# Neighbourhood attention and a mixture of experts: keys and queries copied from their staging tiles straight into the matmul operands, with six key slots

## What is computed

```python
# block 1: 7x7 neighbourhood attention, 12 heads of 32, 16 register tokens
qkv = _gn(x) @ qkv_w.T + qkv_b                  # group norm, 32 groups
reg_kv = registers @ qkv_w[384:].T + qkv_b[384:]
scores = q . concat(k, reg_k) / sqrt(32)        # masked: 7x7 window + 16 registers
x = x + softmax(scores) @ concat(v, reg_v) @ out_w.T + out_b
# block 2: mixture of 4 experts, top 2, hidden width 96
combine = top-2 weights of softmax(xn @ router_w.T + router_b), renormalised
h = gelu(xn @ fc1_w.T + fc1_b)                  # exact gelu, xn = _gn(x)
x = x + (h * combine) @ fc2_w + combine @ fc2_b
```

## Time and profile before

| what | us |
|---|---|
| three runs of the kernel | 646.35, 649.06, 655.0 (median 649.06) |
| span of the profiled execution (first to last instruction) | 648.7 |
| PE busy in it | 570.3 (88%) |
| DVE busy | 447.4 (69%) |
| ACT busy | 308.6 (48%) |
| POOL busy | 294.5 (45%) |
| q1 (SP's DMAs): packets, MB, share of 16 engines | 121032, 73.85, 43.4% |
| q0 (POOL's DMAs) | 9504, 18.84, 9.4% |

### The profile page before, as it was taken

One profiled execution on the slowest core, in us unless ns is written; L12 is line 12 of the kernel. 1 busy time (PEld: TensorE's weight loads), 2 busy tenths in 40 slices (PEclk: granted clock), 3 DMA queues, 4 the chain that ended last, 5 costly groups with the idle time before them and its releaser, 6 DMA issues.

```text
span 648.7 us, 22391 instructions
## 1 busy us (share of the span) xinstructions
PE 570.3 (88%) x9227; PEld 399.9 (62%) x9227; DVE 447.4 (69%) x1009; ACT 308.6 (48%) x609; POOL 294.5 (45%) x433
## 2 busy tenths in 40 slices
PE   3578779999899988998999988898887889998998
PEld 2336666667665866667776776655765656665554
DVE  6885575777887777775667777876688796873333
ACT  1762455215634298512663145451588337754221
POOL 3116699155222667435993362223757232313131
PEclk8799999999999998998999999899998899999999
DMA  9769674995339952397527955179651002121213
GB/s 305 181 153 287 170 203 142 222 282 152 102 77 238 242 150 67 86 261 210 154 59 172 270 170 158 33 181 264 178 141 46 3 0 74 39 74 37 74 37 109
DMA packets 130636, 94.10 MB, mean 145 GB/s; under 512 B 67132, under 2 KB 124392, under 8 KB 130536
## 3 DMA queue, kind: packets, MB, share of 16 engines
q1 hardware_dynamic: 121032, 73.85, 43.4%
q0 software_dynamic: 9504, 18.84, 9.4%
HBM read 56.29 MB, written 35.54 MB: 142 GB/s over the span
## 4 chain that ended last, share of the span: by engine, by line
PE 63%; DVE 12%; ACT 6%; issue 6%; DMA 5%; SPq 4%; POOL 3%; POOLq 0%; ACTq 0%; DVEq 0%
PE ps L1065 44%; PE ps L1229 6%; PE ps L1180 5%; PE ps L1206 4%; SPq L267 3%; DVE ST L450 2%; ACT PT L885 2%; DVE MX L558 2%; DMA QS<-MT 2%; DMA KB<-kscr 1%; ACT XH L826 1%; DMA X<-in_x 1%; SPq L250 1%; POOL vscr L361 1%; POOL X L390 1%
## 5 line engine op out<-in xcount | busy, mean ns | idle before, releaser
L558 DVE TENSOR_REDUCE MX<-ps 128x2 f32<-128x372 f32 x216 | 108.2, 540 | 65.9 <-PE ps L1180 65.2
L1065 PE MATMUL ps<-XH,WQ 128*128 128x384 f16 x810 | 142.1, 330 | 8.6 <-DVE XH L499 7.7
L1065 PEld LDWEIGHTS ps<-XH,WQ 128*128 128x128 f16 x810 | 78.0, 99 | 63.6 <-ACT XH L826 7.6
L885 ACT ACTIVATE PT<-ps 128x448 f32<-128x448 f32 (+1 forms) x162 | 78.6, 511 | 40.1 <-PE ps L1206 39.9
L1206 PE MATMUL ps<-QS,KB 122*128 122x112 f16 (+1 forms) x864 | 65.3, 215 | 18.2 <-ACT PT L885 11.9
L430 POOL TENSOR_TENSOR KT<-QS,KT 128x384 f16<-128x384 f32 x36 | 34.3, 963 | 97.2 <-ACT KT L978 97.2
L1180 PE MATMUL ps<-KB,QS 120*32 120x186 f16 x1728 | 57.4, 250 | 17.7 <-issue 6.9
L1206 PEld LDWEIGHTS ps<-QS,KB 122*128 122x128 f16 x864 | 44.1, 100 | 39.5 <-ACT PT L885 20.7
L1065 PE MATMUL ps<-WQ,XH 128*128 128x128 f16 x972 | 62.5, 223 | 4.5 <-issue 4.2
L1065 PEld LDWEIGHTS ps<-WQ,XH 128*128 128x128 f16 x972 | 56.3, 100 | 10.3 <-issue 8.1
L1229 PE MATMUL ps<-PT,VR 128*32 128x112 f32 (+1 forms) x1296 | 61.2, 263 | 1.1 <-DMA VR<-vscr 0.6
(11 more groups left out here) (168 smaller groups left out, 1005.5 us busy)
## 6 DMA issues: line engine op xcount, KB each, us to landing
KB<-kscr SPq DMA_DIRECT2D x108, 192.0 KB, 4.6
kscr<-KT SPq DMA_DIRECT2D x72, 192.0 KB, 2.5
VR<-vscr SPq DMA_DIRECT2D x216, 56.0 KB
QS<-qscr SPq DMA_DIRECT2D x108, 96.0 KB, 5.8
out<-X SPq DMA_DIRECT2D x11, 576.0 KB, 3.3
X<-in_x SPq DMA_DIRECT2D x6, 576.0 KB, 7.3
qscr<-QT POOLq DMA_DIRECT2D x18, 192.0 KB, 3.1
qscr<-PT POOLq DMA_DIRECT2D x18, 192.0 KB, 5.0
```

Source lines behind the costliest of these rows:

```text
L558: V.tensor_reduce(out=MX[:, s % 2, t, 2 * pair:2 * pair + 2], in_=ps[:, S_BANK(s, i), 0:2 * RUN].rearrange("p (h n) -> p h n", h=2), op=AL ...
L885: A(PTS[n % 4][:, 0:w], ps[:, ST_BANK(n), 0:w], ACT.Exp, scale=SCORE).then_inc(s_["exd"], 1)
L1065: last = mm(bank, lhsT(a, k), rhs(b, k), start=(k == 0 and n == 0), stop=(finish and k == steps - 1 and n == 2))
```

## The change

- The channels of queries and keys are permuted within each group of 128 (by the host, in weights and biases), so that partition `4 d + h` holds channel `d` of head `h`. A staging tile then has the same order of elements as the operand's 32 partitions by four heads.
- `kscr` and `qscr` are gone. After each strip SP copies the KT slot into KB with three DMAs, each 192 KB in 768 runs of 256 bytes (128 keys), to all six tiles at once. `queries_in` copies the QTS slot into QS with three DMAs of 96 KB each, in runs of 768 bytes.
- KB has six slots instead of four (L59), so that the reload of tiles 4 and 5 in the loop goes. Two more copies of the key table are loaded at the start.
- The wait for the last key scores of the stage before (`st_mm`) now stands before the first strip's copy. DVE waits before it reuses a KT slot for three DMAs into KB (`kb_in`) instead of two into `kscr`. ACT waits for `qs_in` instead of `q_out`. PE waits before the stage's first scores for all 18 key DMAs, instead of tile by tile.
- POOL's six query DMAs of each stage are gone.
- The scratch for descriptors of POOL's DMAs is set to 4096 bytes, where it had its default.

```diff
-        KB = sb("KB", [P, HEADS, 4, SLOTW], F16)
+        KB = sb("KB", [P, HEADS, STRIPS, SLOTW], F16)
...
-            for i in range(4):
+            for i in range(STRIPS):
                 sp.dma_start(KB[96:TROWS, :, i, :], ktab.unsqueeze(1).broadcast_to([26, HEADS, SLOTW])).then_inc(s_["t_in"], 16)
...
-            def keys_out(gi, a):
+            def keys_in(gi, a):
                 sp.wait_ge(s_["k_lo"], 6 * gi + a + 1)
                 sp.wait_ge(s_["krg"], 3 * gi + 3)
-                for part in range(2):
-                    sp.dma_start(kscr[part, :, :, a, :], KT[:, a % 3, part, :, :]).then_inc(kw_out[a % 3], 16)
-
-            def keys_in(gi, s):
+                if 36 * gi > 0:
+                    sp.wait_ge(s_["st_mm"], 36 * gi)
                 for j, part in enumerate((0, 1, 0)):
-                    sp.dma_start(KB[DH * j:DH * (j + 1), :, slot(s), LEAD:LEAD + STRIPS * CHUNK],
-                                 kscr[part, :, s, :, :].rearrange("(h d) a n -> d h (a n)", d=DH)).then_inc(kb_in[slot(s)], 16)
+                    sp.dma_start(KB[DH * j:DH * (j + 1), :, :, LEAD + CHUNK * a:LEAD + CHUNK * (a + 1)],
+                                 KT[:, a % 3, part, :, :]).then_inc(kb_in[a % 3], 16)
 
             def queries_in(gi, s):
-                sp.wait_ge(q_out[s], 16 * (gi + 1))
+                sp.wait_ge(s_["q_lo"], 6 * gi + s + 1)
                 for j, part in enumerate((0, 0, 1)):
-                    sp.dma_start(QS[DH * j:DH * (j + 1), :, s * SN:(s + 1) * SN],
-                                 qscr[part].rearrange("(h d) n -> d h n", d=DH)[:, :, s * SN:(s + 1) * SN]).then_inc(qs_in[s], 16)
+                    sp.dma_start(QS[DH * j:DH * (j + 1), :, s * SN:(s + 1) * SN], QTS[s % 5][:, part, :]).then_inc(qs_in[s], 16)
...
                 for a in range(STRIPS):
-                    keys_out(gi, a)
-                for i in range(3):
-                    sp.wait_ge(kw_out[i], 64 * gi + 64)
-                if gi == 0:
-                    sp.wait_ge(s_["t_in"], 16 * 5)
-                if 36 * gi > 0:
-                    sp.wait_ge(s_["st_mm"], 36 * gi)
-                for s in range(4):
-                    keys_in(gi, s)
-                    queries_in(gi, s)
-                for s in (4, 5):
+                    keys_in(gi, a)
+                for s in range(TILES):
                     queries_in(gi, s)
...
-                    if s < 2:
-                        sp.wait_ge(s_["st_mm"], 36 * gi + 6 * (s + 1))
-                        keys_in(gi, s + 4)
                     values_in(gi, s + 2)
...
-            def queries_out(gi, s):
-                pool.wait_ge(s_["q_lo"], 6 * gi + s + 1)
-                pool.dma_start(qscr.rearrange("a p n -> p a n")[:, :, s * SN:(s + 1) * SN], QTS[s % 5]).then_inc(q_out[s], 16)
...
-                if 64 * gi + 32 * (a // 3) > 0:
-                    dve.wait_ge(kw_out[a % 3], 64 * gi + 32 * (a // 3))
+                if 96 * gi + 48 * (a // 3) > 0:
+                    dve.wait_ge(kb_in[a % 3], 96 * gi + 48 * (a // 3))
...
                 if s == 5:
-                    act.wait_ge(q_out[0], 16 * (gi + 1))
+                    act.wait_ge(qs_in[0], 48 * (gi + 1))
...
                 for i in ((2,), (3,), (4,), (0, 1, 5))[n] if n < 4 else ():
-                    act.wait_ge(q_out[i], 16 * (gi + 1))
+                    act.wait_ge(qs_in[i], 48 * (gi + 1))
...
                 if i == 0:
-                    pe.wait_ge(kb_in[slot(s)], kb_count(gi, s))
                     pe.wait_ge(qs_in[s], 48 * (gi + 1))
+                    if s == 0:
+                        for j in range(3):
+                            pe.wait_ge(kb_in[j], 96 * (gi + 1))
+                        if gi == 0:
+                            pe.wait_ge(s_["t_in"], 16 * (STRIPS + 1))
...
+    turned = np.arange(P).reshape(HEADS, DH).T.reshape(-1)
...
-    nc = bacc.Bacc("TRN2", target_bir_lowering=False, num_devices=1)
+    nc = bacc.Bacc("TRN2", target_bir_lowering=False, num_devices=1, dynamic_dma_scratch_size=4096)
```

More of the change, by code:

```diff
@@ L43, in query_rows @@
     return max(0, 8 * a - 3), min(H, 8 * a + 11)
-def slot(s):
-    return s % 4
 def build(nc, x, wqkv, wo, fc1, fc2, rw, cst, fb2, qtab, ktab, gdown, gup, ident16, tri, pick, out):
@@ L138, in build @@
         CS = [q16[:, N:N + TOK * 96].rearrange("p (t n) -> p t n", t=TOK), ptf[:, 0:TOK * 96].rearrange("p (t n) -> p t n", t=TOK)]
-        qscr = nc.dram_tensor("qscr", [2, P, N], F16, kind="Internal").ap()
-        kscr = nc.dram_tensor("kscr", [2, P, TILES, STRIPS, CHUNK], F16, kind="Internal").ap()
         vscr = nc.dram_tensor("vscr", [H, PADW, P], F32, kind="Internal").ap()
@@ L183, in build @@
         v_out = [sem(f"v_out{i}") for i in range(TILES)]
-        q_out = [sem(f"q_out{i}") for i in range(TILES)]
         vr_in = [[sem(f"vr_in{i}{j}") for j in (0, 1)] for i in (0, 1)]
-        kw_out = [sem(f"kw_out{i}") for i in range(3)]
-        kb_in = [sem(f"kb_in{i}") for i in range(4)]
+        kb_in = [sem(f"kb_in{i}") for i in range(3)]
         qs_in = [sem(f"qs_in{i}") for i in range(TILES)]
-        def kb_count(gi, s):
-            if s in (2, 3):
-                return 48 * (gi + 1)
-            return 96 * gi + (48 if s < 2 else 96)
         K_BANK = (4, 6, 2, 3, 5, 7)
@@ L296, in _ @@
                             sp.wait_ge(v_out[i], 48 * STAGES)
+                        for i in range(3):
+                            sp.wait_ge(kb_in[i], 96 * STAGES)
                         for src, dst in ((fc2, f2raw), (rw, rwraw)):
@@ L344, in register_keys @@
                 for i in range(3):
-                    if 64 * gi > 0:
-                        pool.wait_ge(kw_out[i], 64 * gi)
+                    if 96 * gi > 0:
+                        pool.wait_ge(kb_in[i], 96 * gi)
                     for part in range(2):
@@ L394, in _ @@
                 register_keys(gi)
-                for s in range(TILES):
-                    queries_out(gi, s)
                 if gi:
@@ L1180, in scores @@
                         last = mm(ps[32 * j:32 * j + 32, S_BANK(s, i), hh * RUN:(hh + 1) * RUN], QS[0:SROWS, h, q0:q0 + 32],
-                                  KB[0:SROWS, h, slot(s), at:at + RUN], start=True, stop=True)
+                                  KB[0:SROWS, h, s, at:at + RUN], start=True, stop=True)
                 last.then_inc(s_["s_mm"], 1)
@@ L1205, in key_scores @@
                 for h in range(HEADS):
-                    last = mm(ps[:, ST_BANK(n), h * w:(h + 1) * w], KB[0:TROWS, h, slot(s), LEAD + CHUNK * a:LEAD + CHUNK * (a + 1)],
+                    last = mm(ps[:, ST_BANK(n), h * w:(h + 1) * w], KB[0:TROWS, h, s, LEAD + CHUNK * a:LEAD + CHUNK * (a + 1)],
                               QS[0:TROWS, h, s * SN + CT_ * q0:s * SN + CT_ * q1], start=True, stop=True)
@@ L1492 @@
     qkv_b = np.asarray(L0_conv_qkv_b)
+    turned = np.arange(P).reshape(HEADS, DH).T.reshape(-1)
     group = np.arange(C) // (C // GROUPS)
     member = (group[:, None] == np.arange(GROUPS)[None, :]).astype(np.float32)
-    consts = [column(qkv_b[:2 * C]), column(qkv_b[2 * C:]), column(L0_conv_out_b), column(np.asarray(L1_conv_fc1_b).reshape(-1)),
+    consts = [column(qkv_b[:2 * C])[turned], column(qkv_b[2 * C:]), column(L0_conv_out_b), column(np.asarray(L1_conv_fc1_b).reshape(-1)),
               np.broadcast_to(np.asarray(L1_conv_router_b).reshape(1, -1), (P, EXPERTS)), flat(np.asarray(L0_conv_registers).T)]
@@ L1501 @@
             pick[row + e, e * HID:(e + 1) * HID] = 1
-    wqkv = np.asarray(L0_conv_qkv_w).reshape(3, KC, P, KC, P).transpose(4, 1, 3, 0, 2).reshape(P, KC, KC * C)
+    wqkv = np.asarray(L0_conv_qkv_w).reshape(3, KC, P, KC, P)
+    wqkv = np.stack([wqkv[0][:, turned], wqkv[1][:, turned], wqkv[2]]).transpose(4, 1, 3, 0, 2).reshape(P, KC, KC * C)
     arrays = {
```

## The result

The changed kernel takes **725.23 us** (median; 722.32 to 727.2 for three of its four runs, the fourth 733.65) where the kernel before takes 649.05 in the same comparison: 1.117 times as long, 95% interval 1.112 to 1.122. The forecast was 643 with a range of 634 to 659, so sign and range are both wrong. The profiled execution of the changed kernel took 727.2 with a span of 725.4, 76.7 more than the span before.

A forecast was written before the change was run, and what follows sets the result against it. TensorE, busy 570.3 of 648.7 us, was taken to bound the kernel. 648.7 + 7.5 (key slots) - 4.0 (KB waits) - 8.3 (issue stops) - 1.0 (half clock) = 642.9, so 643 us, range 634 to 659.

The forecast's parts named there:

- c: Time of one key DMA from SBUF into KB after the change, taken as 0.75 us, bounds 0.58 and 0.92.
- The 338 GB/s: Rate of one stretch of reads into the same 32 partitions; put 196.6 KB at 0.58 us, the lower bound.
- The rule on ports: Skill page: 32 neighbouring partitions reach half of 16 DMA ports; 0.90 us a key DMA, loss 14.3 us.
- The double-price rival: A key copy in 256-byte pieces costs double, 1.42 us; loss 37.7, issue stops stay, 682 us; chance 6 in 100.
- The formula of the ring: Three key slots: third query product can start 3.0 + 9c us after SP's first issue; loss 7.5 us in all.
- the queries' landing: ScalarE's wait for first queries in QS: covered, 129.6 against 132.45; at 0.92 a key DMA, 0.4 us a stage.
- the clock: TensorE's half-clock stretch after the stop of stage 3, 1.3 us: 1.0 us taken back, bounds 0 and 1.3.
- Stage 0: No loss taken there from the key slots, since a product has 2 us on average.
- The threshold of 0.88: Time of one key DMA, in us, from which the kernel would be slower than before.
- KB's wait: TensorE's 5.0 us wait for KB goes with the reload; gain 4.0 after VectorE's maxima, bounds 2.0 and 5.0.
- Issue: TensorE's issue stops, 11.1 us: 8.3 gained if full engines cause them; rival that they stay, 652, 20 in 100.
- The scratch: Smaller descriptor scratch taken as 0; rival that it holds POOL up, 8 us on the path, 651, 3 in 100.

The follow-up runs named there:

- the scratch run: The kernel before with only the descriptor scratch set to 4096 bytes: 648.42 us, ratio 0.995.
- the two last runs: Direct key copies tile by tile, four slots, to neighbouring rows: 691.14 us; the same with SP sending fewer key and query copies at a time: 700.55 us.

## Why the prediction was wrong, point by point

**c, the price of one key DMA, is the step that failed.** I took 0.75 us from the write to DRAM in the same pieces and kept 0.92 as the upper end. Alone it costs 1.90. In the kernel, by my own formula, 3.0 + 9c = 143.61 - 124.06 gives c = 1.84. Both bounds were rows of other paths: the write has another target, and the reads into the same partitions have DRAM as their source and pieces of 1536 bytes. The experiments split it: the same copy to 128 partitions is at most 0.93, other sets of 32 bring 1.90 to 1.19 and less, longer pieces to 1.45, DRAM as the source to 1.22. No row of before had all three properties together, and the bound from "the nearest rows, however far" was too low by half.

**The 338 GB/s was misread.** In the 0.8 us of that row only 1536-byte pieces of the keys moved, but it is the fastest stretch of a transfer: from first packet to last the three reads took 2.96 us, 0.99 each, so that even for that path 0.58 was no bound. (The 277 GB/s that I gave for the writes is 196.6 KB in 0.71 us; 1.48 MB in 5.4 us are 274.)

**The rule on ports** was given as an estimate of 0.90 and held back because of that row. The Trainium skill, "SBUF — State Buffer", "Door 1: The DMA port swizzle", has about 436 GB/s for all 16 ports, of which I took half as an estimate. The direction was right, the size wasn't: the copy ran at 196.6 KB / 1.90 us = 103 GB/s.

**The double-price rival**, 682, had the right sign, and its price of 1.42 was still too low. Its reason was the piece size. The measured effect of that is 1.90, 1.57 and 1.45 us for pieces of 256, 512 and 1536 bytes to 32 neighbours, and no doubling at 512. The copy to 128 partitions can't tell, since its issues alone take 0.75 of its 0.93. The Trainium skill, "DMA: Bandwidth & Descriptors", "Specifications", has transfers below 512 bytes read, modified and written; no run here shows such a step.

**The formula of the ring held.** With the 1.90 of the copies alone it puts the third query product 3.0 + 17.1 = 20.1 us behind SP's first issue; in stages 1 to 5 it starts 19.6, 19.8, 19.2, 21.1 and 19.6 behind. The loss by it is 45 x 1.90 - 26.25 = 59.3, and the ring's stops in these stages are 34.6 + 19.9 = 54.5. But with this c my whole sum gives 648.7 + 59.3 - 4.0 - 8.3 - 1.0 = 694.7, still 31 short of 725.4. **Two terms that I put at nothing or better make up most of that**: the queries' landing, some 15 us on TensorE, and the clock, taken as 1.0 us better, where the stops of each stage brought half clock behind them, 19.5 us of busy time. **Stage 0 isn't free** either (9.9 us lost). Its slack of 2 us a product doesn't cover nine DMAs at 1.8 (waits for QT 1.2 us, for XH 3.5 more than before), and 7.1 of its loss are the queries' landing. The threshold of 0.88 was not tested; at 1.19 the kernel is 26 us slower.

**What goes.** KB's wait went (5.0, right; VectorE's maxima took back 1.7, 4.5 us in place of 2.8, where I had 1.0). Issue fell by 8.2 (8.3 forecast), though with the engines fuller than before, not emptier: not my reason, and so the number was luck: the scratch run alone lies 2.9 us off the kernel before. With direct queries alone issue fell by 10.6 and the time stayed, so that the gain is not shown to be worth its size either. In this kernel the ring keeps few copies under way, as I read it; the two last runs show what a long queue of them does. That every stop of before has the same cause is made likely by the packets that precede their ends; no run tests it.

**What was said to cost nothing.** The scratch: right. The queries' landing: wrong, ScalarE waits 31.3 us for QS, in five places of up to 9.3, because the queries lie behind the slow keys; it was covered only for c up to 0.9, and a query DMA itself takes 0.61 us alone (3.66 for six) where I had 0.375. SP's wait for `st_mm` ahead of the first strip: its waits there end with POOL's register keys, never with TensorE's last key scores, as forecast. Those register keys came 1.0 us later in stage 1 than before (SP's first issue 5.3 us into the stage in place of 4.3).

**What would show it.** SP's time to the last landing was to be 15.3, at most 18.3; its issues alone spread over 26.7. VectorE's waits before the copies of stage 3 were to be 1.8 and about 1.1 us each; they are 5.7, 3.9 and 3.9. The wait in front of the third query product was to be near 1 us and I am wrong "if over 3": 3.88, after 6.8 us of stops for KU.

## What to carry to other kernels

When a copy gets a new path, bound its price by a row that shares source, target partitions and piece size; where there is none, measure six of them alone before the ring of buffers behind them is sized. A copy within SBUF to 32 partitions should be written to every third or fourth one (1.19 and 0.93 us against 1.90 here), which costs an index. Count what slow copies keep the DMA engines from, the code of the engines and the next entries of the queue included; look whether the removal of a reload through DRAM gains anything at all (here, with six slots, the ratios were 1.006 and 1.031).

## What the hardware showed that I had not expected

- SBUF to SBUF from 128 partitions to 32 neighbours runs at 103 GB/s in 256-byte pieces (to 64 neighbours 98) and at 136 in 1536-byte pieces (1.45 us), where DRAM to the same 32 partitions reaches 161 (1.22 us) and 210 (0.93 us). Why it is so much slower than from DRAM is open. From 32 partitions to the same 32 it was 7.31 us for six, faster than from 128 (11.44), so the source partitions have a part in it, and it is not the target alone.
- Instructions come in packets of 16 KB on a queue of their own (q8), 73 in each of these kernels, over the same DMA engines. That they are TensorE's is inferred: its stops end 1.2 to 1.8 us after such a packet, and with a short queue of the same copies they are gone. One came 7.6 us later (36.0 against 28.4 us behind the begin of the stage's key products) when many slow copies were queued. The profile calls the stop "issue" and names no DMA.
- The stops brought half clock behind them (after 3.88 us of standing still nine matmuls took 3.06 us in place of 1.63, granted clock 0.50), so that slow copies also cost busy time: 589.8 us against 570.3.
